# A graph transformer layer on one core: two query tiles turned over in a row, and the orders that follow

## The chip, the cores and the metric

The kernel runs on one core of one Trainium2 chip. The metric is the device time of one execution in microseconds. It is given as the median of three executions, and beside it stands one execution that the hardware profiler recorded.

## What is computed

One transformer layer with a per-batch additive bias, over 16 batches of 512 tokens with 384 features, in float32. The reference, cut to what matters:

```python
D_MODEL, NHEADS, D_FF = 384, 8, 1536            # x: (16, 512, 384), attn_bias: (16, 512, 512)
q, k, v = (split_heads(x @ w + b) for w, b in ((wq, bq), (wk, bk), (wv, bv)))
scores = jnp.einsum('bhqd,bhkd->bhqk', q, k) * dh ** (-0.5) + attn_bias[:, None, :, :]
attn = jax.nn.softmax(scores, axis=-1)
ctx = jnp.einsum('bhij,bhjd->bhid', attn, v)     # back to (b, n, d)
x1 = _rmsnorm(x + ctx @ wo + bo, alpha1, gamma1)
y = _rmsnorm(x1 + jax.nn.silu(x1 @ w1 + b1) @ w2 + b2, alpha2, gamma2)
out = _layernorm(x + y)
```

## The kernel before

The work has two phases. `attention_phase` goes over the 16 batches and writes each batch's unnormalised attention product to `ctx_dram`; `feed_forward_phase` then does the output projection, the two norms and the feed-forward part of every batch. The last attention batch (`LAST`) is a seam: the output projection and first norm of batch 0 are woven into it, in places that the attention's own projections leave free. The change lies in the attention phase alone.

Float32 products are made of split operands: each operand is the sum of a high part (rounded to the matmul's type) and a low part (the rest). ScalarE makes the high part out of a PSUM bank, and VectorE makes the low part after it out of the same bank. So every bank is read twice, by ScalarE and then by VectorE, before TensorE may write it again. The names are `pT_high`/`pT_low` for the transposed probabilities, `project_hi`/`project_lo` (called as `high("q0")`, `low("q0")`) for the q and k projections, and `v_hi`/`v_lo` for the values.

One batch has 8 heads. One head has 4 query tiles of 128 rows. For each head TensorE does these steps, which the text below calls by short names:

- S(h), `scores`: 8 matmuls (lines 1368 and 1375) into four banks `ps_s`, one for each query tile. It waits until the heads' stacked q and k are in place, among it until GpSimd has copied the last 16 rows of the head to where they are needed (`tails_copied`).
- T(h, qt), `transpose_probs`: the probabilities of one query tile are turned over by 4 matmuls of 128 columns (line 1383) into one of two banks `ps_t`, by `qt % 2`. It waits for `exp_done` of this tile, and for `pT_lo_done` of the tile two before it, which had the same bank.
- begin(h) and end(h): the two halves of the product with the values, 4 matmuls each (line 1396), into one of two shared banks `ps_g`.

Between these steps stand, in fixed places of each batch, the projections of the values (`value(0)` to `value(3)`, 9 matmuls of 384 columns each) and six projections of q and k (9 matmuls of 512 columns each, line 1340). `k2` is the last one that reads this batch's `xT`; `q0`, `k0`, `q1`, `k1` and `q2` belong to the next batch already. The values, the projections and the products share the two banks `ps_g`; `SHARED_USES` is the list from whose places `shared_bank` derives the bank and `use_before` the wait.

VectorE adds the bias to the scores and takes the row maximum (`logits`, line 1090), ScalarE takes the exponent (`exponent`, line 839). After the product ScalarE copies the bank to `ctx_stage` (line 243), and SyncE stores it from there.

The order of all engines is written out by hand in the five `batch` functions; every engine works strictly through its own list. Two lists are not in the diff but matter to it:

- SyncE (lines 519, 248, 493, 497): for each projection it issues 6 to 14 copies that stack the projected rows by head (`stack_projection`), and between these the stores of the product and the loads of `xT` and of the bias. From `q0` on it reads: stack q0, stack k0, store(3), stack q1, store(4), the two loads of the next batch's bias into `adj_s`, store(5), stack k1, and then the next batch.
- GpSimd: in each batch it waits for `k2` to be done, splits the next batch's `xT` (line 684 casts, line 676 subtracts, three times), copies the tails of heads 5, 6 and 7 of this batch, then those of heads 0 and 1, and 2, 3 and 4 of the next one (`copy_tails`, lines 694, 698, 704: one, three and three copies for each head). The tails of head 2 need the stack of k1. In the last batch but one, the division of batch 0's product by its sums stands ahead of the tails of heads 2 to 4 (`divide_context` and `add_bo`, lines 267, 272 and 297); it waits for the four reciprocals that VectorE makes there (`invert`, line 262).

Of the kernel before, what the change touches and what calls it, by code (L numbers as in the profile page):

```python
# [23 lines left out]
B, N, D = 16, 512, 384  # L24
H = 8
DH = D // H
F = 1536
TT = N // P
KT = D // P
# [63 lines left out]
def is_rest(t, h):  # L93
# [22 lines left out]
SHARED_USES = ["pv7", "v0", "v1", "v2", "v3", "pv0", "k2", "pv1", "pv2", "q0", "k0", "pv3", "q1", "pv4", "k1", "pv5",  # L116
               "q2", "pv6"]
# [3 lines left out]
def left_out(step, b):  # L121

    if not isinstance(b, int):
        return False
    if b == 0 and step in ("pv7", *VALUES):
        return True
    return b == LAST and step in PROLOGUE_USES
# [9 lines left out]
def shared_bank(step, prologue=False):  # L137
    return PROLOGUE_USES.index(step) % 2 if prologue else (SHARED_USES.index(step) + 1) % 2


def value_bank(b, h):
    at = shared_bank(f"pv{h}")
    return 1 - at if isinstance(b, int) and b == LAST and h >= H - 2 else at


def use_before(step, b):
# [5 lines left out]
    if isinstance(b, int) and b == 0:  # L152
        return PROLOGUE_USES[shared_bank(step)::2][-1], 0
# [209 lines left out]
def attention_phase(nc, shared, x, xT, adj, wq, bqT, wk, bkT, wv, bvT, wo, bo, w1, b1T, alpha1, gamma1,  # L363
                    ctx_dram):
    ctx = ExitStack()
    with ctx:  # L366
# [385 lines left out]

# [50 lines left out]
        def _(act):  # L803
# [59 lines left out]
            def batch(b, first=False, last=False):  # L863
# [10 lines left out]
                else:  # L874
                    pT_high(b, 0, 0)
                    stage_context(b - 1, 6)
                    exponent(b, 1, 0)
                    pT_high(b, 0, 1)
                    stage_context(b - 1, 7)
                    pT_high(b, 0, 2)  # L880
                    v_hi(b, 0)
                    pT_high(b, 0, 3)
                    v_hi(b, 1)
                    exponent(b, 1, 1)

                    pT_high(b, 1, 0)
                    exponent(b, 1, 2)
                    pT_high(b, 1, 1)
                    v_hi(b, 2)
                    exponent(b, 1, 3)  # L890
# [3 lines left out]
                if not first:  # L894
                    exponent(b, 2, 0)
                    exponent(b, 2, 1)

                pT_high(b, 2, 0)
                exponent(b, 2, 2)
                exponent(b, 2, 3)  # L900
                if not first:
                    high("k2")
                pT_high(b, 2, 1)
                if first:
                    xT_high(1, 0)
                    xT_high(1, 1)
                else:
                    stage_context(b, 0)
                if last:
                    context(0)  # L910
                pT_high(b, 2, 2)
                if first:
                    xT_high(1, 2)
                exponent(b, 3, 0)
                pT_high(b, 2, 3)
                exponent(b, 3, 1)
                exponent(b, 3, 2)

                if last:
                    pT_high(b, 3, 0)  # L920
                    exponent(b, 3, 3)
                    context(1)
                    pT_high(b, 3, 1)
                    context(2)
                else:
                    exponent(b, 3, 3)
                    pT_high(b, 3, 0)
                    pT_high(b, 3, 1)
                exponent(b, 4, 0)
                stage_context(b, 1)  # L930
                pT_high(b, 3, 2)
                exponent(b, 4, 1)
                pT_high(b, 3, 3)
                exponent(b, 4, 2)
                exponent(b, 4, 3)

                pT_high(b, 4, 0)
# [5 lines left out]
                high("k0")  # L943
                pT_high(b, 4, 3)
                square(0)
                exponent(b, 5, 1)
                stage_context(b, 3)

                pT_high(b, 5, 0)
# [3 lines left out]
                exponent(b, 6, 0)  # L953
                square(1)
                high("q1")
                pT_high(b, 5, 2)
                exponent(b, 6, 1)
                pT_high(b, 5, 3)
                exponent(b, 6, 2)
                stage_context(b, 4)  # L960
                exponent(b, 6, 3)

                pT_high(b, 6, 0)
                if last:
                    last_heads()
                    return
                pT_high(b, 6, 1)
                exponent(b, 7, 0)
                pT_high(b, 6, 2)
                pT_high(b, 6, 3)  # L970
                exponent(b, 7, 1)
                high("k1")
                exponent(b, 7, 2)
                exponent(b, 7, 3)

                pT_high(b, 7, 0)
                pT_high(b, 7, 1)
                stage_context(b, 5)
                exponent(b + 1, 0, 0)
                exponent(b + 1, 0, 1)  # L980
                pT_high(b, 7, 2)
                exponent(b + 1, 0, 2)
                pT_high(b, 7, 3)
                high("q2")
                exponent(b + 1, 0, 3)

            def first_heads():
# [8 lines left out]
                project_hi(0, "k", 2, shared_bank("k2"))  # L996
# [9 lines left out]

            def last_heads():
                shared.first_square(act, 0, 2)
                pT_high(LAST, 6, 1)
                exponent(LAST, 7, 0)  # L1010
                pT_high(LAST, 6, 2)
                exponent(LAST, 7, 1)
                pT_high(LAST, 6, 3)
                shared.first_square(act, 0, 3)

                pT_high(LAST, 7, 0)
                exponent(LAST, 7, 2)
                stage_context(LAST, 5)
                pT_high(LAST, 7, 1)
                exponent(LAST, 7, 3)  # L1020
                pT_high(LAST, 7, 2)
                pT_high(LAST, 7, 3)
# [33 lines left out]
        def _(dve):  # L1056
# [44 lines left out]
            def batch(b, first=False, last=False):  # L1101
# [17 lines left out]
                else:  # L1119
                    pT_low(b, 0, 0)  # L1120
# [941 lines left out]
```

## Time and profile before

| | |
|---|---|
| median of 3 executions | 1909.93 us (1909.55 to 1911.77) |
| the profiled execution | 1909.8 us, of which 1907.8 us are the span of the profile |
| TensorE busy | 1882.7 us, 99% of the span |
| VectorE, ScalarE, GpSimd busy | 1334.2, 1143.3 and 1128.9 us (70%, 60%, 59%) |
| granted TensorE clock | 0.999 over the span |
| one attention batch, from one batch's step to the same step of the next | 60.1 us |
| attention phase | about 990 us of the span |

The engines' shares are means over both phases. The profile's times are in microseconds from the start of the span. Its matmul rows overlap, because a matmul's row lasts until its result has drained; what a matmul costs TensorE is the distance from its start to the start of the next. A bracket at the end of a row gives how long the engine had stood idle before it, and whose work ended that.

### The profile page before, as it was taken

What the parts mean: (1) busy time and instruction counts of PE and PEld (TensorE: products, weight loads), DVE (VectorE), ACT (ScalarE), POOL (GpSimd) and SP (SyncE); (2) the same over time, 40 slices, a digit from 0 to 9 for tenths busy, and PEclk for the clock granted to TensorE, in tenths of its full rate; (3) what the DMA queues carried; (4) which work ended last, traced back from release to release, by engine and by line L of the source; (5) the groups of instructions that cost most, each with busy time, mean ns of one, the idle gap of its engine ahead of it and who ended that gap; (6) DMA issues with size and microseconds to landing.
All of it is one profiled execution on the core that took longest, in us unless ns stands there. A gap on an engine that the chain in (4) does not pass through costs nothing. (4 is left out here: it accounts for less than half of the span.)

```text
span 1907.8 us, 39560 instructions
## 1 busy us (share of the span) xinstructions
PE 1882.7 (99%) x10336; PEld 1601.6 (84%) x10336; DVE 1334.2 (70%) x2583; ACT 1143.3 (60%) x2059; POOL 1128.9 (59%) x1735
## 2 busy tenths in 40 slices
PE   7999999999999999999999999999999999999998
PEld 6777787777777777777779999999999999999997
DVE  6777777777777777777786666665566665566754
ACT  5777777777777777777784444433444433444432
POOL 4655544655446554465687766667666667756653
PEclk9999999999999999999999999999999999999999
DMA  5545554455454554565552222211222211222101
GB/s 162 144 130 158 151 151 130 135 152 155 136 145 135 150 158 125 150 174 152 162 156 94 89 88 88 81 48 51 84 88 88 81 45 54 84 88 88 39 20 42
DMA packets 118474, 212.26 MB, mean 111 GB/s; under 512 B 19488, under 2 KB 48672, under 8 KB 116512
## 3 DMA queue, kind: packets, MB, share of 16 engines
q1 hardware_dynamic: 118432, 211.77, 36.7%
q8 instruction: 18, 0.29, 0.1%
q14 instruction: 24, 0.20, 0.0%
HBM read 106.83 MB, written 41.94 MB: 78 GB/s over the span
## 5 line engine op out<-in xcount | busy, mean ns | idle before, releaser
L1097 DVE TENSOR_TENSOR pT_lo<-ps_t,pT_hi 128x512 fp32r<-128x512 f32 x512 | 349.1, 687 | 96.0 <-ACT pT_hi L846 94.2
L846 ACT ACTIVATE pT_hi<-ps_t 128x512 fp32r<-128x512 f32 x512 | 303.3, 596 | 141.4 <-PE ps_t L1383 138.0
L839 ACT ACTIVATE probs<-probs,neg_max 128x512 f32<-128x512 f32 x512 | 357.5, 721 | 32.7 <-DVE neg_max L1090 31.7
L1383 PE MATMUL ps_t<-ident,probs 128*128 128x128 f32 x2048 | 311.3, 276 | 7.1 <-DVE pT_lo L1097 4.4
L1383 PEld LDWEIGHTS ps_t<-ident,probs 128*128 128x128 f32 x2048 | 241.5, 140 | 90.6 <-issue 32.4
L1090 DVE CUSTOM_DVE_ANT_0 probs<-ps_s,adj_s 128x512 f32<-128x512 f32 x424 | 278.9, 684 | 54.9 <-PE ps_s L1375 23.1
L1903 DVE TENSOR_TENSOR h_lo<-hidden,h_hi 128x512 fp32r<-128x512 f32 x192 | 171.4, 893 | 166.4 <-ACT h_hi L1810 166.3
L698 POOL CAST tails<-k_wide 16x512 fp32r<-16x512 f32 x384 | 233.9, 609 | 50.6
L2007 PE MATMUL ps_y<-w_hi,h_hi 128*128 128x384 f32 x768 | 258.3, 336 | 0.0
L2007 PE MATMUL ps_y<-w_hi,h_lo 128*128 128x384 f32 x768 | 257.2, 335 | 0.0
L2007 PE MATMUL ps_y<-w_lo,h_hi 128*128 128x384 f32 x768 | 257.1, 335 | 0.0
L694 POOL CAST k_wide<-k_wide 32x512 fp32r<-32x512 f32 x128 | 78.2, 611 | 293.7 <-DMA k_wide<-weights_hi 276.2
L1965 PE MATMUL ps_h<-in_hi,weights_hi 128*128 128x512 f32 x576 | 225.4, 391 | 0.3 <-PEq L366 0.3
L1965 PE MATMUL ps_h<-in_hi,weights_lo 128*128 128x512 f32 x576 | 225.1, 391 | 0.0
L1965 PE MATMUL ps_h<-in_lo,weights_hi 128*128 128x512 f32 x576 | 224.4, 390 | 0.0
L1396 PE MATMUL ps_g<-pT_hi,v_s 128*112 128x512 f32 x512 | 221.8, 433 | 0.1
L1802 ACT ACTIVATE hidden<-ps_h,b_c 128x512 f32<-128x512 f32 x192 | 131.7, 686 | 136.2 <-PE ps_h L1965 136.2
L1789 ACT ACTIVATE squares<-y 128x384 bf16<-128x384 f32 x64 | 33.5, 524 | 290.9 <-DVE y L1851 290.9
L1396 PE MATMUL ps_g<-pT_lo,v_s 128*112 128x512 f32 x512 | 201.8, 394 | 0.0
L1368 PE MATMUL ps_s<-k_wide,q_wide 128*128 128x512 f32 x512 | 150.1, 415 | 1.0 <-DVE neg_max L1090 1.0
L704 POOL CAST q_tails<-tails 16x128 fp32r<-16x128 f32 x384 | 110.3, 287 | 57.7 <-DMA q_wide<-wo_hi 4.5
L2007 PEld LDWEIGHTS ps_y<-w_lo,h_hi 128*128 128x128 f32 x768 | 144.3, 188 | 0.0
(120 smaller groups left out, 4010.5 us busy)
## 6 DMA issues: line engine op xcount, KB each, us to landing
ctx_dram<-ctx_stage SPq DMA_DIRECT2D x128, 224.0 KB
ctx_raw<-ctx_dram SPq DMA_DIRECT2D x15, 1792.0 KB, 7.3
k_wide<-weights_hi SPq DMA_DIRECT2D x188, 96.0 KB, 2.3
q_wide<-weights_lo SPq DMA_DIRECT2D x188, 96.0 KB, 2.3
adj_first<-in_adj SPq DMA_DIRECT2D x30, 512.0 KB, 6.7
adj_s<-in_adj SPq DMA_DIRECT2D x30, 512.0 KB, 6.5
rows<-in_x SPq DMA_DIRECT2D x16, 768.0 KB, 6.1
z<-in_x SPq DMA_DIRECT2D x16, 768.0 KB, 4.7
```

The costliest lines, as they stand in the source:

```text
L698: pool.tensor_copy(tail(tails, g)[:, h, :], wide_of["k"][TAIL:DH, h, :]).then_inc(tails_copied, 1)
L839: nc.scalar.activation(probs[:, at, :], probs[:, at, :], ACT.Exp, scale=-1.0, bias=neg_max[:, at:at + 1]).then_inc(exp_done, 1)
L846: nc.scalar.activation(pT_hi[:, h % 2, qt, :, :], ps_t[qt % 2][:, :].rearrange("p (k i) -> p k i", k=TT), ACT.Copy)\
L1090: nc.vector.tensor_tensor_reduce(out=probs[:, at, :], in0=ps_s[qt][:, :], in1=rows, scale=-1.0, scalar=BIG, op0=ALU.add, op1=ALU.min, accu ...
L1097: nc.vector.tensor_tensor(pT_lo[:, h % 2, qt, :, :].rearrange("p k i -> p (k i)"), ps_t[qt % 2][:, :], pT_hi[:, h % 2, qt, :, :].rearrange ...
L1368: nc.tensor.matmul(ps_s[qt][:, :], lhsT=wide_of["q"][:, h, toks], rhs=wide_of["k"][:, h, :], start=True, stop=False)
L1383: last = nc.tensor.transpose(ps_t[qt % 2][:, kt * P:(kt + 1) * P], probs[:, ring(h, qt), kt * P:(kt + 1) * P], ident[:, :])
L1396: last = nc.tensor.matmul(out, lhsT=v_head, rhs=pT[:, :, kt, :], start=(kt == 0 and part == 0), stop=(kt == TT - 1 and part == 1))
L1802: nc.scalar.activation(hidden[:, j % BUFS, :], ps_h[j % BUFS][:, :], ACT.Silu, bias=b1_c[:, j:j + 1]).then_inc(hidden_ready, 1)
L1903: nc.vector.tensor_tensor(h_lo[:, j, :], hidden[:, j % BUFS, :], h_hi[:, j, :].bitcast(FP32), ALU.subtract).then_inc(h_lo_done, 1)
L1965: last = nc.tensor.matmul(out_ps, lhsT=lhsT, rhs=rhs, start=(n == 0), stop=(n == 3 * len(pairs) - 1))
L2007: end = nc.tensor.matmul(ps_y[t % 2][:, 0:D], lhsT=lhsT, rhs=rhs, start=(n == 0), stop=(n == 3 * JT - 1))
```

## The change

The head's steps on TensorE get another order. Before, each tile's transposition was followed by something else: T(h,0), S(h+1), T(h,1), a projection, T(h,2), begin, T(h,3), end. After, two tiles are turned over in a row: T(h,0) T(h,1), S(h+1), a projection or begin, T(h,2) T(h,3), end (or begin and end). In head 1 of a batch this puts S(2) ahead of `value(2)` and `value(3)`; `k2` moves behind S(3), and `k0` behind the product of head 3. The lists of ScalarE and VectorE are rewritten to match: `pT_high(h,2)`, `pT_high(h,3)`, then the two exponents of the next head, then `stage_context`; on VectorE the last two `logits` of a head come after `pT_low(h-1,3)`. `SHARED_USES` is rearranged so that all products but the first use one shared bank and all projections the other. The special lists of the last batch (`last_heads`) go, and the steps of the seam stand inside the common list. The number of matmuls, activations, vector operations and transfers stays as it was. The lists of SyncE and GpSimd stay too, but for one wait in the last batch.

```diff
-SHARED_USES = ["pv7", "v0", "v1", "v2", "v3", "pv0", "k2", "pv1", "pv2", "q0", "k0", "pv3", "q1", "pv4", "k1", "pv5",
-               "q2", "pv6"]
+SHARED_USES = ["pv7", "v0", "v1", "v2", "v3", "pv0", "pv1", "k2", "pv2", "q0", "pv3", "k0", "pv4", "q1", "pv5", "k1",
+               "pv6", "q2"]
...
@@ scalar, batch
                 pT_high(b, 4, 0)
-                stage_context(b, 2)
-                high("q0")
-                pT_high(b, 4, 1)
+                exponent(b, 4, 2)
+                pT_high(b, 4, 1)
+                high("q0")
+                exponent(b, 4, 3)
                 pT_high(b, 4, 2)
+                pT_high(b, 4, 3)
                 exponent(b, 5, 0)
...
+                high("k1")
+                square(2)
                 pT_high(b, 6, 2)
                 pT_high(b, 6, 3)
+                exponent(b, 7, 0)
                 exponent(b, 7, 1)
+                stage_context(b, 5)
+                square(3)
...
@@ vector, batch
-                logits(b + 1, 0, 0)
-                logits(b + 1, 0, 1)
                 pT_low(b, 7, 0)
-                logits(b + 1, 0, 2)
                 pT_low(b, 7, 1)
-                logits(b + 1, 0, 3)
-                invert(0, 3)
+                if last:
+                    shared.first_scale(dve, 0, 3)
+                else:
+                    logits(b + 1, 0, 0)
+                    logits(b + 1, 0, 1)
+                    low("q2")
                 pT_low(b, 7, 2)
                 pT_low(b, 7, 3)
-                low("q2")
+                if last:
+                    return
+                logits(b + 1, 0, 2)
+                logits(b + 1, 0, 3)
+                invert(0, 2)
+                invert(0, 3)
...
@@ tensor, batch
                     transpose_probs(b, 0, 0)
+                    transpose_probs(b, 0, 1)
                     scores(b, 1)
                     begin(7)
-                    transpose_probs(b, 0, 1)
+                    end(7)
                     transpose_probs(b, 0, 2)
-                    end(7)
+                    transpose_probs(b, 0, 3)
                     value(0)
-                    transpose_probs(b, 0, 3)
                     value(1)
 
                     transpose_probs(b, 1, 0)
+                    transpose_probs(b, 1, 1)
+                    scores(b, 2)
                     value(2)
-                    transpose_probs(b, 1, 1)
                     value(3)
                     transpose_probs(b, 1, 2)
-                    scores(b, 2)
                     transpose_probs(b, 1, 3)
                     begin(0)
                     end(0)
 
                 transpose_probs(b, 2, 0)
+                transpose_probs(b, 2, 1)
+                scores(b, 3)
                 if not first:
                     projection("k2")
-                transpose_probs(b, 2, 1)
-                scores(b, 3)
                 transpose_probs(b, 2, 2)
+                transpose_probs(b, 2, 3)
                 begin(1)
-                transpose_probs(b, 2, 3)
                 end(1)
...
                 transpose_probs(b, 4, 0)
+                transpose_probs(b, 4, 1)
                 scores(b, 5)
-                transpose_probs(b, 4, 1)
-                projection("k0")
+                begin(3)
                 transpose_probs(b, 4, 2)
-                begin(3)
                 transpose_probs(b, 4, 3)
                 end(3)
+                projection("k0")
```

## Rows read from the trace of the kernel before

**Rows 1.** The head of the page: the span, and the engines' busy time.
```profile
span 1907.8 us, 39560 instructions
...
PE 1882.7 (99%) x10336; PEld 1601.6 (84%) x10336; DVE 1334.2 (70%) x2583; ACT 1143.3 (60%) x2059; POOL 1128.9 (59%) x1735
```

**Rows 2.** Waits from 60 to 900 us: total, times, longest us.
```profile
PE ps_t L1383 <- DVE pT_lo L1097: 2.5, 14, 0.2
```

**Rows 3.** TensorE's timeline (start, us, instruction): eight transpositions, then products.
```profile
328.46 1.04 PE L1383 MATMUL ps_t<-ident,probs 128*128 128x128 f32 x8
329.25 0.47 PE L1396 MATMUL ps_g<-pT_hi,v_s 128*112 128x512 f32 x1
329.56 0.39 PE L1396 MATMUL ps_g<-pT_lo,v_s 128*112 128x512 f32 x1
329.79 0.40 PE L1396 MATMUL ps_g<-pT_hi,v_s 128*112 128x512 f32 x1
```

**Rows 4.** TensorE's timeline, same batch: T(1,0), and S(2).
```profile
333.83 0.60 PE L1383 MATMUL ps_t<-ident,probs 128*128 128x128 f32 x4
...
338.23 1.17 PE L1368 MATMUL ps_s<-k_wide,q_wide 128*128 128x512 f32 x4
```

**Rows 5.** GpSimd's timeline: tails of head 2; xT split; last copies of head 5.
```profile
331.48 0.61 POOL L694 CAST k_wide<-k_wide 32x512 fp32r<-32x512 f32 x1 [12.73 <-DMA k_wide<-weights_hi]
...
334.44 1.12 POOL L704 CAST q_tails<-tails 16x128 fp32r<-16x128 f32 x3
...
344.93 0.61 POOL L684 CAST in_hi<-rows 128x512 fp32r<-128x512 f32 x1 [0.94 <-PE ps_g L1340]
...
354.29 1.12 POOL L704 CAST q_tails<-tails 16x128 fp32r<-16x128 f32 x3
```

**Rows 6.** SyncE's queue: first copies of stack q0, and stack k1.
```profile
360.09 1.85 SPq L519 DMA_DIRECT2D q_wide<-weights_lo  x3
...
385.00 5.25 SPq L519 DMA_DIRECT2D k_wide<-weights_hi  x8
```

**Rows 7.** ScalarE's timeline after q0: pT_high(4,0), stage_context(2), high q0.
```profile
357.58 0.60 ACT L846 ACTIVATE pT_hi<-ps_t 128x512 fp32r<-128x512 f32 x1 [0.65 <-PE ps_t L1383]
358.07 0.59 ACT L243 ACTIVATE ctx_stage<-ps_g 112x512 f32<-112x512 f32 x1
358.55 0.69 ACT L816 ACTIVATE weights_lo<-ps_g,bq_c 128x512 fp32r<-128x512 f32 x1
```

**Rows 8.** VectorE's timeline, the same moment: low q0.
```profile
359.27 0.75 DVE L1062 SCALAR_TENSOR_TENSOR weights_lo<-ps_g,bq_c,weights_lo 128x512 fp32r<-128x512 f32 x1 [0.37 <-ACT weights_lo L816]
```

**Rows 9.** TensorE's timeline: T(2,1); last product, T(3,0); T(4,0); S(5).
```profile
344.63 0.60 PE L1383 MATMUL ps_t<-ident,probs 128*128 128x128 f32 x4
...
349.07 0.40 PE L1396 MATMUL ps_g<-pT_lo,v_s 128*112 128x512 f32 x1
349.64 0.63 PE L1383 MATMUL ps_t<-ident,probs 128*128 128x128 f32 x4 [0.17 <-DVE pT_lo L1097]
...
356.86 0.60 PE L1383 MATMUL ps_t<-ident,probs 128*128 128x128 f32 x4
357.22 1.17 PE L1368 MATMUL ps_s<-k_wide,q_wide 128*128 128x512 f32 x4
```

**Rows 10.** ScalarE's timeline: high k2, pT_high after it; two exponents in a row.
```profile
344.99 0.69 ACT L816 ACTIVATE weights_hi<-ps_g,bk_c 128x512 fp32r<-128x512 f32 x1 [0.34 <-PE ps_g L1340]
345.58 0.59 ACT L846 ACTIVATE pT_hi<-ps_t 128x512 fp32r<-128x512 f32 x1
...
355.59 1.34 ACT L839 ACTIVATE probs<-probs,neg_max 128x512 f32<-128x512 f32 x2
```

**Rows 11.** VectorE's timeline in the last batch but one: the last reciprocal.
```profile
926.47 0.95 DVE L262 RECIPROCAL inv_sum<-ctx_raw 128x128 f32<-128x128 f32 x1
```

**Rows 12.** GpSimd's timeline there: division; tails of the last batch's head 2.
```profile
927.50 3.77 POOL L272 TENSOR_TENSOR ctx_raw<-ctx_raw,inv_sum 128x512 f32<-128x512 f32 x3 [3.33 <-DVE inv_sum L262]
...
935.95 0.60 POOL L694 CAST k_wide<-k_wide 32x512 fp32r<-32x512 f32 x1 [0.80 <-DMA k_wide<-weights_hi]
```

More of the change, by code:

```diff
@@ L124, in left_out @@
         return False
-    if b == 0 and step in ("pv7", *VALUES):
+    if b == 0 and step in ("pv7", "k2", *VALUES):
         return True
@@ L893, in batch @@
                     pT_high(b, 1, 3)
-                if not first:
                     exponent(b, 2, 0)
                     exponent(b, 2, 1)
+                    stage_context(b, 0)
                 pT_high(b, 2, 0)
+                pT_high(b, 2, 1)
+                if first:
+                    xT_high(1, 0)
                 exponent(b, 2, 2)
+                if first:
+                    xT_high(1, 1)
                 exponent(b, 2, 3)
@@ L902, in batch @@
                     high("k2")
[L903 to L910, printed above, removed]
                 pT_high(b, 2, 2)
+                pT_high(b, 2, 3)
                 if first:
@@ L1142, in batch @@
                 pT_low(b, 2, 0)
-                if not first:
-                    low("k2")
                 pT_low(b, 2, 1)
@@ L1147, in batch @@
                 logits(b, 3, 1)
+                if not first:
+                    low("k2")
+                pT_low(b, 2, 2)
+                pT_low(b, 2, 3)
                 logits(b, 3, 2)
-                pT_low(b, 2, 2)
                 logits(b, 3, 3)
-                pT_low(b, 2, 3)
+                pT_low(b, 3, 0)
+                pT_low(b, 3, 1)
+                logits(b, 4, 0)
                 if last:
@@ L1185, in batch @@
+                pT_low(b, 5, 1)
                 logits(b, 6, 0)
                 logits(b, 6, 1)
-                pT_low(b, 5, 0)
-                pT_low(b, 5, 1)
+                low("q1")
+                pT_low(b, 5, 2)
+                pT_low(b, 5, 3)
                 logits(b, 6, 2)
-                if last:
-                    last_heads()
-                    return
                 logits(b, 6, 3)
-                pT_low(b, 5, 2)
-                low("q1")
-                pT_low(b, 5, 3)
@@ L1197, in batch @@
                 invert(0, 0)
-                logits(b, 7, 0)
-                logits(b, 7, 1)
                 pT_low(b, 6, 0)
                 pT_low(b, 6, 1)
-                invert(0, 1)
+                logits(b, 7, 0)
+                if last:
+                    shared.first_scale(dve, 0, 0)
+                logits(b, 7, 1)
+                low("k1")
+                pT_low(b, 6, 2)
+                pT_low(b, 6, 3)
                 logits(b, 7, 2)
                 logits(b, 7, 3)
-                pT_low(b, 6, 2)
@@ L1207, in batch @@
-                pT_low(b, 6, 3)
-                low("k1")
-                invert(0, 2)
-                logits(b + 1, 0, 0)
-                logits(b + 1, 0, 1)
+                invert(0, 1)
+                if last:
+                    shared.first_scale(dve, 0, 1)
+                    shared.first_scale(dve, 0, 2)
                 pT_low(b, 7, 0)
-                logits(b + 1, 0, 2)
                 pT_low(b, 7, 1)
-                logits(b + 1, 0, 3)
-                invert(0, 3)
+                if last:
+                    shared.first_scale(dve, 0, 3)
[3 more added lines that the diff above has]
+                    low("q2")
```

185 lines of the change are left out of this document (67 added, 118 removed).

## The prediction, made before the changed kernel ran

> **What bounds the kernel now.** I read the page's head first: TensorE is busy for 99% of the span, every other engine for 70% or less [rows 1]. So only TensorE's own line counts, and an edit can do three things: change what a matmul costs by its neighbours, take away a wait of TensorE, or put in a new one. Next the waits: between 60 and 900 us TensorE waits for one thing only, `pT_low`, 14 times, once a batch [rows 2]. Its timeline shows where: T(3,0) starts 0.57 us after the last matmul of end(1), where the next start is usually 0.23 us on [rows 3, 9]. That is 0.34 us lost a batch, some 4.8 us in 14 batches; there is no more waiting for a new order to remove in the loop. Last I read, for every S(h), how long the tails of its head had been ready, because the order moves S against GpSimd and SyncE, whose lists stay.
>
> **The price of turning two tiles over in a row.** A transposition of one tile is four matmuls. The trace has them in runs of eight already: from the first to the product behind it 0.79 us, so about 0.11 us for each and 0.03 for the last; the product's first matmul then takes 0.31 instead of 0.23 [rows 3]. Together 0.87 us over eight, 0.11 each. A run of four gives the same: S(5) starts 0.36 us after T(4,0) [rows 9]. So I price the pairing itself at nothing. Sixteen runs fewer a batch could be worth up to 0.08 us each if the slow step behind a run were the run's alone; by the same rows it is made up for by the 0.03, so I take 0, with bounds of 0 and 1.3 us a batch gained.
>
> The Trainium skill (TensorE: Matmul & The Clock Gate, Back-to-back issue gap) gives 81 ns as the sustained pace of weight load and matmul at 128 columns. If only long runs reached it, 1,920 transpositions would give back 54 us by that page. The run of eight here stands at 109 ns a matmul [rows 3], against it.
>
> **S(2), the term that decides.** Before, T(1,0), value(2), T(1,1), value(3) and T(1,2) stand ahead of S(2): 333.83 to 338.23, 4.40 us. After, only T(1,0) and T(1,1) do: 0.79 us, so TensorE wants S(2) at 334.62, 3.61 us earlier [rows 3, 4]. It waits for the tails of head 2. GpSimd ends these at 334.44 + 1.12 = 335.56, and it could not begin before 331.48, because it had waited 12.73 us for the stack of k1 to land [rows 5]. That margin was 2.67 us and is less than 3.61. It is 2.57 to 2.85 in 11 of the loop's batches, 2.2 and 2.0 in batches 2 and 14, and 5.6 in batch 1.
>
> The chain behind it gets longer too. SyncE issues the stack of k1 at 385.00 at the end of a row of copies that began with the stack of q0 at 360.09, 25 us without a stop for TensorE [rows 6]; it began as soon as low q0 had ended, 359.27 + 0.75 [rows 8]. Before, ScalarE ran `pT_high(4,0)`, `stage_context(2)`, `high q0`: 357.58, 358.07, 358.55 [rows 7]. After, `exponent(4,2)` (0.62) and `pT_high(4,1)` (0.48) stand between, in place of `stage_context` (0.48), so high q0 starts about 0.6 us later and low q0 with it [rows 7, 8, 10]. All of SyncE's row, the loads of the bias and the landing move by it: bounds 0 (if the queue has a pause that I don't see) and 0.7, I take 0.6. From GpSimd's end to TensorE's start I take 0.1 us; VectorE's reciprocal to GpSimd took 0.08, high to low 0.03 [rows 7, 8, 11, 12]; bounds 0.03 and 0.25.
>
> So S(2) starts at 335.56 + 0.6 + 0.1 = 336.26, 1.64 us after TensorE is free for it. Everything on TensorE is queued behind it: value(2) and value(3), both T of head 1, and with them all of the batch. It comes back each time, since SyncE's row starts from q0, which TensorE does after S(2). Other waits between q0 and the next S(2) are covered by this one.
>
> **The other waits, in the same batch.** T(3,0) gets rid of its 0.34 us: VectorE now does `pT_low(2,2)` ahead of the last two `logits`. But T(h+1,1) becomes tight after each projection. Counted from the start of T(h,2): high starts at 0.36, `pT_high(h,2)` at 0.95, `pT_high(h,3)` at 1.43, the two exponents of the next head at 1.92 and 2.54, the second ends at 3.26 [rows 7, 9, 10]. TensorE needs 0.79 for the run and 0.31 + 7 x 0.23 = 1.92 for the product, and wants T(h+1,0) at 2.71 and T(h+1,1) at 3.15 [rows 3]. With 0.1 on top, T(h+1,1) waits 0.2 us (bounds 0 and 0.4). There are four such places a batch; the three of heads 5, 6 and 7 lie between q0 and S(2), under the wait above. T(3,1) counts: +0.2.
>
> S(5) had 357.22 - 355.41 = 1.81 us of margin [rows 5, 9]. k2, from whose end GpSimd's chain starts (344.93 [rows 5]), moves behind T(2,1) and S(3), some 2.0 us, and S(5) by one T, 0.44. The margin is about 0.1 us or nothing; it too lies under the wait at S(2). Tails of the other heads have over 3 us left.
>
> The shared banks cost nothing as I see it. Between two uses of one bank lie at least T, T and S, 0.79 + 1.17 = 1.96 us; a stage needs about 0.36 + 0.6, and q1 after low k0 needs 0.36 + 0.69 + 0.75 + 0.1 = 1.9 [rows 3, 4, 8, 10]. If that cover goes, it is some tenths a batch.
>
> One loop batch: 1.64 + 0.20 - 0.34 = 1.5 us. Eleven of them: 16.5 us. Batch 2 and 14 with their smaller margins: 2.0 and 2.15. Batch 1 keeps its margin and pays 0.4 for small waits. Batch 0: 0, bounds -1 and +1.
>
> **The last batch.** Here the tails of head 2 stand behind the division, and that waits for the last reciprocal (GpSimd idle for 3.33 us, start 927.50) [rows 12]. VectorE did it at 926.47, 1.56 us after T(7,2) [rows 11]. Now low q2, two `pT_low`, two `logits` and one reciprocal precede it: from T(7,2) 1.08 + 0.66 + 4 x 0.61 + 0.87, about 5.0 us. So it is 3.5 us later, the 0.80 us that GpSimd still waited for the landing fall away [rows 12], and the tails come about 2.8 us later. S(2) had 2.2 us of margin and goes 3.61 forward: 3.61 - 2.2 + 2.8 + 0.1 = 4.3 us. For the rest of the seam (the split of batch 0's context, the last residual and its norm, in a new order) I have no row that settles it: bounds -1 and +4, I take +1.5.
>
> **Sum.** 16.5 + 2.0 + 2.15 + 0.4 + 4.3 + 1.5 = 26.9 us. The profiled execution took 1909.8 us, the median is 1909.93: 1909.8 + 26.9 = 1936.7, so 1937. The feed-forward phase has the same list and stays.
>
> **Rivals.**
> 1. *The wait at S(2) is smaller.* If low q0 delays nothing and some of SyncE's row has play, each batch loses 0.6 to 1.0 us less: 13 x 0.8 = 10 us less, and the last batch 2 less: 1918 to 1926.
> 2. *The tails come in time, faster.* S(2) doesn't wait if the stack of k1 lands 1.6 us sooner, that is if GpSimd's wait of 12.73 us follows TensorE's pace. Then only the 0.34 us go: 1909.8 - 4.8 = 1905. Against it: SyncE's list is unchanged, and its row is full of copies of 0.6 us each.
> 3. *ScalarE and VectorE become the bound.* With each projection followed by two `pT_high` and two exponents, every one of four T(h+1,1) waits 0.5 us or more, outside the shadow of S(2) too, and `logits` hold up S: 0.8 us more a batch, 15 x 0.8 = 12: 1949 and above. For it: the chain of 3.26 us against 3.15 is tight already. It decides once an exponent starts 0.3 us late.
> 4. *Long runs go faster*, by up to half of 0.109 us for each of 1,920 transpositions: up to 100 us; the row of eight speaks plainly against it.
> 5. *Nothing measurable*: a small wait at S(2), 0.3 us, equals the stall removed: 1906 to 1914.
>
> **Chances.** Forecast (1926 to 1948) 0.68; rival 1, 0.13; rival 2, 0.06; rival 3, 0.06; rival 4, 0.01; rival 5, 0.06. A measurement of this kernel can tell about 0.2%, 4 us. Slower: 0.68 + 0.13 + 0.06 = 0.87; the same 0.06; faster 0.07. The range takes in rival 1, and the bounds of the latencies and the seam: 1918 to 1949.
>
> **What would show it.** Right: in the timeline a gap of some 1.6 us ahead of S(2) in each batch from 2 on, T ahead of it, with the tails of head 2 ending just before; GpSimd's wait for the stack of k1 as long as before, measured on a period that is 61.6 instead of 60.1 us; runs of eight transpositions at 0.79 us; no stall at T(3,0); a gap of over 4 us before S(2) of the last batch. Wrong: S(2) right behind T(1,1). Then the tails were early, and rival 2 or 5 holds. Gaps at T(h,1) of half a microsecond mean rival 3.

## The result, and the profile of the changed kernel

The changed kernel takes 1946.32 us (median of 4, 1945.12 to 1948.56); the kernel before, run beside it, takes 1910.16. The ratio is 1.0192, 95% interval 1.018 to 1.0204. So it is slower by about 36 us, where 27 were forecast (1937, range 1918 to 1949).

The page of after, its head and three groups (columns as in [rows 1]; in a group: busy and mean of one, then the idle time ahead and what ended most of it):

```profile
span 1943.2 us, 39588 instructions
...
PE 1903.5 (98%) x10336; PEld 1608.8 (83%) x10336; DVE 1333.0 (69%) x2583; ACT 1125.2 (58%) x2059; POOL 1131.6 (58%) x1735
...
L1337 PE MATMUL ps_t<-ident,probs 128*128 128x128 f32 x2048 | 278.7, 276 | 9.2 <-ACT probs L839 7.6
...
L694 POOL CAST k_wide<-k_wide 32x512 fp32r<-32x512 f32 x128 | 78.0, 609 | 278.6 <-DMA k_wide<-weights_hi 260.2
...
L1322 PE MATMUL ps_s<-k_wide,q_wide 128*128 128x512 f32 x512 | 151.1, 416 | 12.5 <-POOL q_tails L704 11.9
```

The matmuls are as many as before; the scores (L1322) now wait for the query tails. The waits of after, from 120 to 840 us (total, times, longest us; TensorE's matmuls, then its weight loads). Before, the only wait of a matmul here was 2.1 us for `pT_lo`, the one of [rows 2]:

```profile
PE ps_s L1322 <- POOL q_tails L704: 5.2, 12, 0.5
PE ps_t L1337 <- ACT probs L839: 0.5, 1, 0.5
...
PEld ps_t L1337 <- ACT probs L839: 17.4, 70, 0.9
PEld ps_s L1322 <- POOL q_tails L704: 8.0, 12, 0.8
PEld ps_t L1337 <- DVE pT_lo L1077: 3.8, 12, 0.3
```

Once a batch, then, for the tails, and a weight load some six times a batch, 0.25 us each, for an exponent (before, three times: 37 waits, 9.1 us in this stretch). A matmul behind such a weight load starts 0.05 to 0.11 us late. TensorE's timeline of one batch shows the first:

```profile
341.84 1.04 PE L1337 MATMUL ps_t<-ident,probs 128*128 128x128 f32 x8
343.38 1.20 PE L1322 MATMUL ps_s<-k_wide,q_wide 128*128 128x512 f32 x4 [0.50 <-POOL q_tails L704]
...
355.40 1.03 PE L1337 MATMUL ps_t<-ident,probs 128*128 128x128 f32 x8
356.19 0.48 PE L1352 MATMUL ps_g<-pT_hi,v_s 128*112 128x512 f32 x1
...
357.90 0.40 PE L1352 MATMUL ps_g<-pT_lo,v_s 128*112 128x512 f32 x1
358.14 1.10 PE L1337 MATMUL ps_t<-ident,probs 128*128 128x128 f32 x7
```

A run of eight takes 0.79 us, as before (355.40 to 356.19), T(3,0) follows its product after 0.24 us (357.90 to 358.14; before 0.57 [rows 9]), and S(2) starts 1.54 us after T(1,0) where 0.79 would do.

**Where the time went.** From the starts of S(2), batch by batch, in both traces. The change moves S(2) 3.61 us forward within the batch, so the sum starts at batch 1 with that added.

```
                              before     after   difference   forecast
S(2) of batch 1 (with 3.61)    97.62     96.01      +2.0        +0.4
period to batch 2              60.18     62.41      +2.2        +2.0
11 periods, to batch 13       661.68    677.33     +15.7       +16.5
period to batch 14             60.56     64.69      +4.1        +2.15
period to the last batch       62.19     69.33      +7.1        +4.3
S(2) to the feed-forward       47.83     55.07      +3.6        +1.5   (less 3.61)
feed-forward to the end       917.77    918.33      +0.6         0
                                                   +35.3       +26.9
```

**The loop, by its chain.** The period is now the way from one S(2) to the next through the other engines. After: ScalarE's high q0 and VectorE's low q0, SyncE's first copy of stack q0 and first of stack k1, GpSimd's first and last copies for head 2:

```profile
367.78 0.70 ACT L816 ACTIVATE weights_lo<-ps_g,bq_c 128x512 fp32r<-128x512 f32 x1
...
368.54 0.74 DVE L1042 SCALAR_TENSOR_TENSOR weights_lo<-ps_g,bq_c,weights_lo 128x512 fp32r<-128x512 f32 x1
...
369.35 1.85 SPq L519 DMA_DIRECT2D q_wide<-weights_lo  x3
...
394.29 5.31 SPq L519 DMA_DIRECT2D k_wide<-weights_hi  x8
...
400.76 0.61 POOL L694 CAST k_wide<-k_wide 32x512 fp32r<-32x512 f32 x1 [12.56 <-DMA k_wide<-weights_hi]
...
403.72 1.12 POOL L704 CAST q_tails<-tails 16x128 fp32r<-16x128 f32 x3
```

GpSimd's row of before that answers to the first copy, one batch behind [rows 5]:

```profile
391.75 0.61 POOL L694 CAST k_wide<-k_wide 32x512 fp32r<-32x512 f32 x1 [12.79 <-DMA k_wide<-weights_hi]
```

Leg by leg, before (with [rows 4, 6, 8]) and after: S(2) to low q0 21.04 and 25.16; to SyncE 0.82 and 0.81; SyncE to the stack of k1 24.91 and 24.94; to GpSimd's copy 6.75 and 6.47; through the tails 4.08 in both (391.75 to 395.83, 400.76 to 404.84). Before that makes 57.60, and TensorE itself took 60.17, so 2.6 were to spare. After it makes 61.46; the next S(2) starts at 404.90, 0.06 us behind, and 61.52 is this batch's period (the mean of the eleven is 61.57, before 60.15). Of the 4.12 us more to low q0, 3.61 are S(2)'s new place and 0.51 the later high q0 with the waits between.

### The profile page after: what moved, and what is told of

It is laid out like the page before. It is cut to its first block and busy times, and to the rows that moved or that the text cites. A ratio compares the mean times of both kernels' runs of the same rounds, so it can differ in the third digit from the quotient of the medians.

```text
span 1943.2 us, 39588 instructions
## 1 busy us (share of the span) xinstructions
PE 1903.5 (98%) x10336; PEld 1608.8 (83%) x10336; DVE 1333.0 (69%) x2583; ACT 1125.2 (58%) x2059; POOL 1131.6 (58%) x1735
## 5 line engine op out<-in xcount | busy, mean ns | idle before, releaser
L1077 DVE TENSOR_TENSOR pT_lo<-ps_t,pT_hi 128x512 fp32r<-128x512 f32 x512 | 336.8, 686 | 103.6 <-ACT pT_hi L846 103.4
L846 ACT ACTIVATE pT_hi<-ps_t 128x512 fp32r<-128x512 f32 x512 | 288.3, 599 | 28.5 <-PE ps_t L1337 28.4
L1337 PE MATMUL ps_t<-ident,probs 128*128 128x128 f32 x2048 | 278.7, 276 | 9.2 <-ACT probs L839 7.6
L1337 PEld LDWEIGHTS ps_t<-ident,probs 128*128 128x128 f32 x2048 | 233.4, 141 | 63.3 <-ACT probs L839 32.6
L1070 DVE CUSTOM_DVE_ANT_0 probs<-ps_s,adj_s 128x512 f32<-128x512 f32 x424 | 274.2, 684 | 14.8 <-PE ps_s L1329 14.8
L1352 PE MATMUL ps_g<-pT_hi,v_s 128*112 128x512 f32 x512 | 215.9, 422 | 0.2 <-ACT ctx_stage L243 0.2
L1322 PE MATMUL ps_s<-k_wide,q_wide 128*128 128x512 f32 x512 | 151.1, 416 | 12.5 <-POOL q_tails L704 11.9
L1962 PEld LDWEIGHTS ps_y<-w_hi,h_hi 128*128 128x128 f32 x768 | 144.2, 188 | 0.0
```

Of the source, the lines that this page charges most:

```text
L846: nc.scalar.activation(pT_hi[:, h % 2, qt, :, :], ps_t[qt % 2][:, :].rearrange("p (k i) -> p k i", k=TT), ACT.Copy)\
L1070: nc.vector.tensor_tensor_reduce(out=probs[:, at, :], in0=ps_s[qt][:, :], in1=rows, scale=-1.0, scalar=BIG, op0=ALU.add, op1=ALU.min, accu ...
L1077: nc.vector.tensor_tensor(pT_lo[:, h % 2, qt, :, :].rearrange("p k i -> p (k i)"), ps_t[qt % 2][:, :], pT_hi[:, h % 2, qt, :, :].rearrange ...
L1322: nc.tensor.matmul(ps_s[qt][:, :], lhsT=wide_of["q"][:, h, toks], rhs=wide_of["k"][:, h, :], start=True, stop=False)
L1337: last = nc.tensor.transpose(ps_t[qt % 2][:, kt * P:(kt + 1) * P], probs[:, ring(h, qt), kt * P:(kt + 1) * P], ident[:, :])
L1352: last = nc.tensor.matmul(out, lhsT=v_head, rhs=pT[:, :, kt, :], start=(kt == 0 and part == 0), stop=(kt == TT - 1 and part == 1))
```

## The experiments

Ratios are to the kernel before, timed on the same chip, with 95% intervals. "Period" is the mean of the eleven distances from one S(2) to the next between the batches 2 and 13. Two theories stand against each other. The first: one moved step, S(2), costs the time, because its tails come from a chain that TensorE can't hurry. The second: the new order as a whole costs it, by many small waits for ScalarE and VectorE.

**S(2) back.** The changed kernel with S(2) behind `value(2)` and `value(3)`, and the two `logits` with it.

```diff
-                    scores(b, 2)
                     value(2)
                     value(3)
+                    scores(b, 2)
```

> The changed kernel with one thing put back: S(2) stands behind value(2) and value(3) again (both T of head 1 stay in a row). Theory (S(2) waits for the tails of head 2, whose pace SyncE's row sets): TensorE wants S(2) 3.15 us later, so its wait of 0.69 us a batch goes, in batch 14 one of 1.5, and in the last batch 3.2 of 5.7 us, with the half-clock stretch behind it (2 us). 12 x 0.69 + 1.5 + 3.2 + 2 = 15 us less: 1931 us; the small waits at T(3,1), T(6,1), T(7,1), T(0,1) stay, period about 60.9 us. Rival (pairs and their chain on ScalarE cost everything): the waits at T grow by what S(2) gives up, 1943 us or more.

Measured 1933.47 us, 1.0123 (1.0107 to 1.014). The period is 60.85, S(2) starts 2.6 us after its tails. 13 us of the 36 come back, and the loop doesn't get back to 60.15. The small waits, 0.8 us a batch, are as long as in after: 0.17 us at each of T(3,1), T(6,1) and T(7,1), 0.10 at T(0,1), 0.05 at each of T(0,0), T(6,0) and T(7,0). All but the first had been under the wait at S(2), and now they stand in the open.

**S(2) forward, alone.** The kernel before with S(2) ahead of the two value products, and of ScalarE's and VectorE's lists only what stands next to it: exponent(1,2) behind `pT_high(1, 1)`, two `logits` ahead of `v_lo(2)`.

```diff
                     transpose_probs(b, 1, 0)
-                    value(2)
                     transpose_probs(b, 1, 1)
+                    scores(b, 2)
+                    value(2)
                     value(3)
                     transpose_probs(b, 1, 2)
-                    scores(b, 2)
```

> The kernel before with one part of the change alone: in head 1 T(1,0), T(1,1), S(2), then value(2), value(3), T(1,2), T(1,3). Theory: S(2) is wanted 3.61 us earlier and its margin was 2.67, so it waits 1.0 us in 11 batches, 1.5 in batches 2, 14 and 15: 11 + 4.5 = 15.5 us more, 1926 us; period 61.1 us. Rival (the order of S(2) is harmless, the cost is in the other heads): 1910 us.

Measured 1936.96 us, 1.0142 (1.0125 to 1.0159), a miss by 11 us: the period is 61.8 and the waits are elsewhere (120 to 840 us):

```profile
PE ps_t L1383 <- ACT probs L839: 9.0, 12, 0.8
PE ps_g L1396 <- DVE v_s L1068: 3.3, 11, 0.3
PE ps_t L1383 <- DVE pT_lo L1097: 2.2, 12, 0.4
PE ps_s L1368 <- POOL q_tails L704: 0.3, 1, 0.3
```

T(1,1) waits for exponent(1,1), which stands behind `v_hi(1)` on ScalarE, and the first product for all four `v_lo`. Both belong to what the change does beside. So the run didn't try the theory; with those two orders mended it does:

```diff
                     v_hi(b, 0)
+                    exponent(b, 1, 1)
                     v_hi(b, 1)
-                    exponent(b, 1, 1)
 ...
-                        pe.wait_ge(v_lo_done, TT * b + TT)
+                        pe.wait_ge(v_lo_done, TT * b + TT // 2)
```

> The kernel before with S(2) of a batch's first head ahead of its four value products, and with the two edits whose lack b_s2_only showed: exponent(b,1,1) ahead of v_hi(1) on ScalarE, and begin(0) waiting only for the v_lo tiles it reads. Theory (the price is S(2) losing the cover of the value products; the two waits of b_s2_only were a lack of supporting orders): T(1,1) (0.97 us a batch) and begin(0) (0.54) lose their waits, S(2) waits about 1.0 us for GpSimd's last query tail in place of the 0.13 of b_s2_only, a period of 61.15 us instead of 61.8, and 1926 us. Rival (other waits of the moved scores take their place): a period of 61.8 us and 1936 us.

Measured 1925.19 us, 1.0079 (1.0064 to 1.0095). The period is 61.1; by the leg sum of before it should be 57.60 + 3.61 = 61.2. What TensorE waits for, in the same stretch:

```profile
PE ps_s L1368 <- POOL q_tails L704: 7.9, 12, 0.9
PE ps_t L1383 <- DVE pT_lo L1097: 1.9, 11, 0.2
```

The move, in the old order of everything else but what supports it, makes 1.0 us a batch, 15 us in all. The first theory holds for this part of the loss.

**The chain, at its head.** The changed kernel with the high and low parts of q0 one transposition sooner.

```diff
                 pT_high(b, 4, 0)
+                high("q0")
                 exponent(b, 4, 2)
                 pT_high(b, 4, 1)
-                high("q0")
```

> The changed kernel with high q0 and low q0 right behind pT_high(4,0) and pT_low(4,0), so some 1.0 us earlier. Theory: SyncE's row, the landing of stack k1 and the tails of head 2 all come earlier, and the wait at S(2) falls from 0.69 to about 0 in each of 12 batches, in batch 14 by 0.7: 9 us less, 1937 us. The last batch stays, there GpSimd's division sets S(2). Rival (the row is not paced by q0 but by TensorE later on, or by the transfers): S(2) still waits 0.6 us or more, 1945 us or more.

Measured 1932.87 us, 1.012 (1.0103 to 1.0137). The chain is shorter by over a microsecond, S(2) starts 0.2 to 0.5 us after its tails without a wait from batch 3 on, and the period is 60.8, as with S(2) back. 13.4 us come back where 9 were expected: one line moved on each of two engines is worth as much as moving S(2).

**The chain, in its middle.** SyncE issues the first part of stack k1 ahead of the bias loads.

```diff
+                    stack_projection(b + 1, "k", 1, b, (0,))
                     load_adj_pair(b + 1, 0)
                     load_adj_pair(b + 1, 1)
                 shared.store_context(sp, ctx_dram, b, 5)
-                stack_next("k", 1)
+                stack_projection(b + 1, "k", 1, b, (1,))
```

> The changed kernel, with SyncE issuing the first part of stack k1 ahead of the eight bias loads instead of behind them. It asks whether the last query tail at S(2) is late because GpSimd's k1 work sits in line ahead of it. Theory (GpSimd's line before the tails is late by the transfers it waits for): the wait at S(2) goes from about 0.7 us a batch to nothing, a period of 60.8 us, and 1933 us. Rival (the tails wait for the stack of q0 only, which stands behind the same SyncE work as before): a period of 61.5 us and 1946 us, or later by up to 1.3 us a batch through the bias loads.

Measured 1943.58 us, 1.0174 (1.0159 to 1.019): neither theory's time, but the trace parts the two. (The bias loads are two, of 512 KB each, not eight; and the profiled execution, 1947.19 us, is the slowest of its four.) GpSimd, ScalarE and TensorE:

```profile
335.04 0.61 POOL L698 CAST k_wide<-k_wide 32x512 fp32r<-32x512 f32 x1 [7.67 <-DMA k_wide<-weights_hi]
...
279.27 0.60 ACT L243 ACTIVATE ctx_stage<-ps_g 112x512 f32<-112x512 f32 x1 [4.65 <-DMA ctx_dram<-ctx_stage]
...
279.92 0.44 PE L1298 MATMUL ps_g<-weights_hi,in_hi 128*128 128x384 f32 x1 [1.41 <-ACT ctx_stage L243]
```

The tails of head 2 start at 335.04 instead of 339.2 and S(2) has 4.4 us to spare: GpSimd's copies were late by the transfer, and the period is 60.9 in eight batches of eleven. In the other three (62.6 to 63.0) the store of head 5, which follows the moved copies and the two bias loads in the queue, lands late: issued at 270.92, it frees its buffer at 279.2, 8.3 us later, where 6.1 us pass in the next batch. ScalarE's `stage_context` waits for that, and TensorE for ScalarE's bank. A third theory, which neither expectation had: the queue's order trades one late transfer for another.

**The small waits.** The changed kernel with exponent(h+1, 0) of heads 3, 6, 7 and 0 ahead of the high part of the projection.

```diff
+                    exponent(b, 3, 0)
                     high("k2")
                 pT_high(b, 2, 2)
                 pT_high(b, 2, 3)
-                exponent(b, 3, 0)
 ...
```

> The changed kernel with the first exponent of the next head moved ahead of high k2, q1, k1 and q2 on ScalarE, where it stands idle for the projection anyway. Theory: the waits at T(h,0) and T(h,1) behind each projection (about 0.9 us a batch) go, but three of the four places lie between q0 and S(2), so the wait at S(2) grows by what they give up; only T(3,1) counts, 0.17 us a batch: period 61.4 instead of 61.55, 1944 us. Rival (the waits add up as they stand): period 60.7, 1934 us or less.

Measured 1948.02 us, 1.0195 (1.0178 to 1.0212), no change against after. The waits trade places (same stretch as above, lines two further down), and the period stays at 61.56:

```profile
PE ps_s L1324 <- POOL q_tails L704: 9.7, 12, 1.2
...
PEld ps_s L1324 <- POOL q_tails L704: 12.6, 12, 1.5
PEld ps_s L1324 <- DVE neg_max L1072: 9.7, 46, 0.2
```

The shadow is shown: what lies between q0 and S(2) costs nothing while S(2) waits. The 0.17 us at T(3,1), ahead of q0, which the theory wanted to see come back, don't: half of them return in S(4) behind it, which now waits for `logits` (1.17 us to its last four matmuls instead of 1.09). **Both together**, S(2) back and the exponents early, asked whether the small waits are worth their 0.7 us a batch once they are in the open.

> The changed kernel with S(2) behind the values and the early exponents. Theory: with S(2) free, nothing covers or replaces the waits at T; all of the 0.9 us a batch less some 0.2 at S(5) go: period 60.1 to 60.2 instead of 60.85, some 9 us less than with S(2) put back alone: 1924 us; the last batch and batch 13 keep their losses. Rival (the pairs need more of VectorE than it has: pT_low is late instead): period 60.7 or more, 1931 us.

Measured 1931.23 us, 1.0111 (1.0094 to 1.0128), against 1933.47 with S(2) back alone; the period is 60.8, not 60.15. In their place come others:

```profile
PEld ps_s L1324 <- DVE neg_max L1072: 9.2, 45, 0.2
PEld ps_g L1296 <- DVE v_s L1050: 4.0, 12, 0.6
```

The scores now wait for VectorE's `logits`, and `value(2)` for a bank that `v_lo(0)` frees behind two `logits`. The rival's time holds and its kind of cause (VectorE), but not its words: no `pT_low` is late in the loop. Of the 0.7 us a batch that stay against 60.15, some 0.3 are TensorE's own (below, at the pairing); the rest is how the new order lies on ScalarE and VectorE together, and moving one step there only moves the wait.

**The last batch.** `invert(0, 2)` and `invert(0, 3)` of batch 14 behind `logits(7, 3)`, so that GpSimd's division starts sooner.

```diff
                 invert(0, 1)
+                invert(0, 2)
+                invert(0, 3)
 ...
-                invert(0, 2)
-                invert(0, 3)
```

> The changed kernel with the last two reciprocals of the last batch but one moved on VectorE behind logits(7,3), some 7 us earlier. Theory: GpSimd's division and with it the tails of the last batch's head 2 come earlier, bounded by the landing of stack k1; TensorE's wait of 5.7 us at S(2) of the last batch falls to under 2.5 us and TensorE's clock doesn't fall to half behind it: 5 us less, 1941 us. Rival (the wait comes from SyncE's row there too): S(2) waits 5 us as before, 1946 us.

Measured 1940.25 us, 1.0155 (1.0138 to 1.0172), 6.1 us less than after. The last period falls from 69.33 to 65.06, S(2) waits 0.22 us, and the stretch behind it is 1.7 us shorter, of which more below. The clock is 1.00 from 959.6 to 974 us; it was 0.50 earlier, from 956.1 to 959.4.

**Batch 13.** The load of batch 0's first context rows behind the stores of batch 13's.

```diff
-                if last_but_two:
-                    ...
-                    load_first_context(0)
                 shared.store_context(sp, ctx_dram, b, 0)
 ...
                 shared.store_context(sp, ctx_dram, b, 1)
+                if last_but_two:
+                    ...
+                    load_first_context(0)
```

> The changed kernel; in batch 13 alone SyncE issues the first load of batch 0's product behind store(0) and store(1) instead of ahead of them. Theory: stage_context(2) of that batch waited 2.87 us for store(0) to land behind this load; without it high q0 and SyncE's row start some 2 us earlier and S(2) of batch 14 too: period of batch 14 under 63 instead of 64.7, 1944 us. Rival (store(0) is late by itself, because the stack of k2 is): no change.

Measured 1944.1 us, 1.0175 (1.0158 to 1.0192), as expected; by itself the 2 us lie at the edge of what can be told apart, but the period to batch 14 falls from 64.69 to 62.84 in the trace (with q0 or the inversions moved it is 64.75 and 64.17).

**The three mends together** (q0, the inversions, the context load).

> The changed kernel with three edits tried one by one, together: query tile 0's high and low parts turned over right behind those of (4,0), invert(0,2) and (0,3) of the last head behind logits(7,3), and the context load of batch 14 behind the two stores. Theory (three separate waits): 1946.3 - 13.4 - 6.1 - 2.2 = 1924.6 us. Rival (the last batch's wait and the context load are covered by the same earlier query tile): 1946.3 - 13.4 = 1932.9 us.

Measured 1925.89 us, 1.008 (1.0064 to 1.0095). The three gains add up but for 1.3 us, so they are three causes. The clock is 1.00 around the last S(2) (940 to 958 us). The changed order is still 16 us behind.

**The one wait that before had.** The kernel before with `pT_low(2, 2)` ahead of `logits(3, 2)`, the part of the change that takes the stall at T(3,0) away; then also `pT_low(3, 1)` ahead of `logits(4, 1)`.

```diff
+                pT_low(b, 2, 2)
                 logits(b, 3, 2)
-                pT_low(b, 2, 2)
 ...
+                    pT_low(b, 3, 1)
                     logits(b, 4, 1)
-                    pT_low(b, 3, 1)
```

> The kernel before with pT_low(2,2) on VectorE ahead of logits(3,2), nothing else. Theory: the one wait of TensorE in the loop, 0.34 us at T(3,0), goes, 14 x 0.34 = 4.8 us less: 1905.3 us, the version that beats both. Rival (logits(3,2) and (3,3) come later and S(4) waits instead): 1908 to 1912 us.

> The kernel before with pT_low(2,2) ahead of logits(3,2), as b_t30, and in heads other than the last also pT_low(3,1) ahead of logits(4,1). Theory (the 0.2 us that b_t30 lost again at T(3,3) is VectorE's logits(4,1) standing ahead of pT_low(3,1)): another 0.2 x 13 = 2.6 us go, a period of 59.8 us, and 1910.6 - 5.3 = 1905.3 us. Rival (the wait moves to the next transposes or to the scores that need logits(4,1)'s banks): 1908 us, as b_t30.

The first measured 1907.95 us, 0.9989 (0.998 to 0.9999): the 0.34 us at T(3,0) go, and 0.2 come back at T(3,3), a period of 60.02. The second measured 1904.12 us, 0.9967 (0.9955 to 0.9979), a period of 59.78. Its page:

```profile
span 1902.4 us, 39560 instructions
...
PE 1880.3 (99%) x10336; PEld 1602.2 (84%) x10336; DVE 1335.2 (70%) x2583; ACT 1144.0 (60%) x2059; POOL 1134.4 (60%) x1735
```

Two `pT_low` moved by one place each make a kernel that is faster than both, by 6 us against before.

## Why the prediction was right, and where it was short

**S(2) and its chain: right.** The forecast period was 60.15 + 1.5 = 61.65; it is 61.57. Each leg stands as priced: 3.61 for the move; about 0.6 of delay at q0, less 0.34 and plus 0.20 for the stalls, which is 0.46 where 0.51 were measured; SyncE's row unchanged. I took 0.1 from GpSimd to TensorE and it is 0.05. The landing of k1 came 0.28 sooner in the batch shown, but only 0.04 in the mean. The sign that I named, a gap of 1.6 us ahead of S(2), did not come: it is 0.7. I had written myself that the waits between q0 and S(2) lie under this one, and did not take them off. They are 0.6 (T(6), T(7) and T(0)), and part of the pairing's cost, next, lies under it too. The run with early exponents shows that only the sum counts.

**The pairing: not quite free.** Eight transpositions take 0.79 us in every run of eight without a wait, as I said. But the 32 tiles of a batch took 11.89 us before, 0.74 for two, and the slow first step behind a run, of which there are fewer now, is as slow behind the scores (335.89 to 336.22 in after). By kind of step, in the mean of eleven batches: the transpositions go from 11.89 to 14.14 us, of which 0.68 is the wait at S(2) and 0.80 the small waits; the products and projections from 35.96 to 35.13, of which 0.34 is the stall at T(3,0); the scores stay. That leaves 0.3 us a batch, 4 us in all, for which I had taken 0 with bounds on the side of a gain. It is read by subtraction; no run tries it alone. The Trainium skill (TensorE: Matmul & The Clock Gate, Back-to-back issue gap) gives 81 ns for a weight load and matmul at 128 columns; by that page the runs would have gained an estimated 50 us. They stand at 109 ns a matmul in both kernels.

**The waits at T(h,1): right in size.** T(3,1), T(6,1) and T(7,1) wait 0.17 us a batch and T(0,1) 0.10, where 0.2 was forecast for each of the four. I had none at T(0,0), T(6,0) and T(7,0), 0.05 each. Together they are the 0.8 us of the forecast, and all but T(3,1) cost nothing only because S(2) waits later. Rival 2 forgot them: "only the 0.34 us go" was wrong, since three different ways to free S(2) end at 60.8 to 60.9, and 60.15 - 0.34 + 0.8 + 0.3 is 60.9. Rival 3 is not it: no place waits the 0.5 us that it wanted.

**Batch 14: the wait right, a cause beside it missing.** 2.28 us of the 4.1 are what was forecast (62.84 - 60.56, with the load moved). The rest is a queue I had looked past. ScalarE and SyncE of after in batch 13:

```profile
859.82 0.60 ACT L243 ACTIVATE ctx_stage<-ps_g 112x512 f32<-112x512 f32 x1 [2.87 <-DMA ctx_dram<-ctx_stage]
...
861.88 0.69 ACT L816 ACTIVATE weights_lo<-ps_g,bq_c 128x512 fp32r<-128x512 f32 x1
...
853.47 0.52 SPq L534 DMA_DIRECT2D ctx_raw<-ctx_dram  x1
854.03 1.70 SPq L248 DMA_DIRECT2D ctx_dram<-ctx_stage  x2
...
863.45 1.86 SPq L519 DMA_DIRECT2D q_wide<-weights_lo  x3
```

`stage_context(2)` now stands ahead of high q0 and of `pT_high(4,0)`, and it needs its staging buffer, which a store frees that lies behind the context load. It waits 1.1 us for that store in the loop, and 2.87 here. High q0 comes 26.13 us after S(2) instead of 24.40, and SyncE's row with it. Of the step I moved I had counted its 0.48 us, not the transfer that it waits for.

**The last batch: right in kind, a term too small.** The reciprocals were to be 3.5 us later by VectorE's own instructions (which less the 0.80 gives 2.7 for the tails, not 2.8); GpSimd's division is 6.1 us later (from S(2) of batch 14: 47.46 before [rows 12]; 57.19 after, less 3.61). ScalarE, GpSimd and TensorE of after:

```profile
952.00 0.69 ACT L816 ACTIVATE weights_lo<-ps_g,bq_c 128x512 fp32r<-128x512 f32 x1 [3.84 <-DMA q_wide<-weights_lo]
...
957.63 3.79 POOL L272 TENSOR_TENSOR ctx_raw<-ctx_raw,inv_sum 128x512 f32<-128x512 f32 x3 [8.92 <-DVE inv_sum L262]
...
965.46 0.60 POOL L694 CAST k_wide<-k_wide 32x512 fp32r<-32x512 f32 x1 [0.16 <-POOL rows L297]
...
954.32 1.26 PE L1337 MATMUL ps_t<-ident,probs 128*128 128x128 f32 x8 [2.14 <-ACT probs L839]
...
963.15 1.18 PE L1337 MATMUL ps_t<-ident,probs 128*128 128x128 f32 x8
969.77 2.04 PE L1322 MATMUL ps_s<-k_wide,q_wide 128*128 128x512 f32 x4 [5.44 <-POOL q_tails L704]
```

High q2 overwrites a tile that SyncE is still copying from for the stack of q1; in the changed kernel it comes early enough to wait for it, 3.84 us. VectorE's low q2, and behind it the reciprocals, wait too. The forecast had only what stands ahead on VectorE, not what that waits for. The landing that GpSimd had waited for fell away as foreseen (0.16).

**The rest of the seam: 3.6 instead of 1.5.** I had no row for it. Two parts can be read:

```profile
PE ps_g L338 <- DVE in_lo L284: 1.8, 1, 1.8
```

is new (waits from 960 to 1030 us); and TensorE's clock. The windows around S(2) (PEclk is the third number from the right):

```profile
960.00:966.00 6.00, 4.33 (x26) 3.58 (x24) 4.06 (x10) 5.18 (x11) 5.84 (x7) 1.00 0.78 229
967.00:973.00 6.00, 3.23 (x10) 1.99 (x11) 0.43 (x1) 0.00 (x0) 4.72 (x10) 0.50 0.40 104
```

S(2) takes 2.70 us to the next product (969.77 to 972.47) where 1.56 is usual (343.38 to 344.94), and three products take 0.5 more: 1.6 us. With the inversions moved the clock is 1.00 there and the same stretch is 1.7 us shorter.

**Batch 0 and 1: 2.0 instead of 0.4.** T(2,2) of batch 0 waits for two exponents of ScalarE, which starts its own order of first heads later than TensorE's new one asks:

```profile
44.97 0.88 PE L1337 MATMUL ps_t<-ident,probs 128*128 128x128 f32 x4 [2.06 <-ACT probs L839]
46.10 1.11 PE L1337 MATMUL ps_t<-ident,probs 128*128 128x128 f32 x4 [0.25 <-ACT probs L839]
```

Behind them the clock is 0.50 from 45.5 to 48.5 us, where before has 1.00. The run of eight takes 1.65 us beside its wait (1.90 less 0.25, usual 0.79), and the product 2.76 (46.87 to 49.63, usual 1.95): 1.7 us, most of the 2.0. It isn't the same each time. Four of the changed kernels have the same instructions up to here, and S(2) of batch 1 starts at 95.08 us in the one whose clock stays at 1.00 (the context load moved), at 96.01 (after) and 96.75 (stack k1 first) with such a stretch, and at 97.62 with one twice as long (the inversions moved). The bounds of -1 and +1 were too narrow, and this row is good to a microsecond or so. No run took it apart; that ScalarE's order of batch 0 sets it off is read from these rows, not shown. The 0.6 us in the feed-forward phase, whose list is the same, are no more than scatter: over all fourteen profiles it takes 917.77 to 918.39 us, and before has the least.

In sum, 26.9 us were forecast and 35.3 are in the traces. The loop came out 0.8 us below its forecast, while every term outside it was too small, and the range held by its upper bounds.

## What to carry to other kernels

When a step is moved forward on the engine that bounds the kernel, follow its input back through every queue until the chain closes on that same engine: the sum of the legs is a second period, and the kernel takes the longer of the two. Take the wait that you see for a sum, since small waits ahead of a large one are paid for by it, and they come out when it is mended. Of a moved step, price also what it waits for (a buffer that a store frees, a tile still being copied), for that is where some four and a half of the eight and a half missing microseconds lay.

## What the runs showed of the hardware

- TensorE's granted clock was 1.00 from 960 to 966 us, and 0.50 (1.2 of 2.4 GHz) from 967 to 973 us, after the engine had stood still since 963.94 us for the tails. It came back to 1.00 in the projections behind (975 to 981 us). A wait of 5.8 us thus cost 7.4. In batch 0 it was 0.50 as well (45.5 to 48.5 us), after waits of 1.35 and 2.06 us close together, and in the run with the inversions moved from 956.1 to 959.4 us, after one of 1.87.
- From the end of GpSimd's last tail to TensorE's start 0.05 to 0.06 us pass in each of the thirteen batches 2 to 14 of after.
- A context store of 224 KB frees its buffer 4.4 us after its issue in the loop (361.33 to 365.7), 5.8 us when a context load of 512 KB was issued 0.56 us ahead of it (854.03 to 859.8), and in one batch 8.3 us behind two bias loads of 512 KB (270.92 to 279.2). An on-chip copy of 96 KB lands in 2.3 us.
  The Trainium skill (DMA: Bandwidth & Descriptors, Anatomy of one DMA, SWDGE (gpsimd) path) puts the fixed cost of a transfer on GpSimd's path at about 2 us and warns of a surprisingly long delay where the target is HBM. The transfers here are issued by SyncE, which that section does not cover; the copies' 2.3 us are near its figure, and the stores to HBM, at 4.4 us and more, are the slower ones, as it says.
